# Octonion FFN kernel: another order of the opening steps, and GpSimd's pairing of the last chunks in two steps

## What is computed

```python
W = weights[condition]
y = einsum('bct,bcd->bdt', x, W)
def ternary_dequant(W):
    scale = mean(abs(W))
    return scale * clip(round(W / scale), -1, 1)
def oct_ternary_linear(xp, W):
    M = einsum('jik,jod->koid', S_OCT, ternary_dequant(W))
    return einsum('...id,koid->...ko', xp, M)
h = silu(oct_ternary_linear(y, w_gate)) * oct_ternary_linear(y, w_up)   # 8 x 341.5 -> 2732 wide
out = x + oct_ternary_linear(h, w_down)
```

## Time and profile before

| | before |
|---|---|
| median of 3 runs | 679.83 us (679.83 to 680.08) |
| the profiled execution | 679.09 us |
| its span | 677.3 us |
| TensorE (PE) busy | 643.8 us, 95% of the span |
| VectorE (DVE) | 516.5 us, 76% |
| GpSimd (POOL) | 385.1 us, 57% |
| ScalarE (ACT) | 323.2 us, 48% |
| TensorE's mean granted clock | 0.986 of full |

### The profile page before, as it was taken

One profiled execution on the slowest core, in us unless ns is written; L12 is line 12 of the kernel. 1 busy time (PEld: TensorE's weight loads), 2 busy tenths in 40 slices (PEclk: granted clock), 3 DMA queues, 4 the chain that ended last, 5 costly groups with the idle time before them and its releaser, 6 DMA issues. The chain is left out here.

```text
span 677.3 us, 17118 instructions
## 1 busy us (share of the span) xinstructions
PE 643.8 (95%) x7010; PEld 595.5 (88%) x7010; DVE 516.5 (76%) x873; ACT 323.2 (48%) x542; POOL 385.1 (57%) x453
## 2 busy tenths in 40 slices
PE   3599899999999999999999999999999999999997
PEld 3378699899999999998998999999999999988986
DVE  1899977868776787868877698767878687787785
ACT  4847455345534545254454446254462545434440
POOL 1256685547637576348646476376754486465553
PEclk9799899999999999999999999999999999999997
DMA  9200030140003200041001300031000300021001
GB/s 345 67 2 1 1 116 15 39 155 1 2 2 102 90 2 2 1 137 55 2 2 61 132 1 2 1 126 68 1 2 6 121 1 2 2 72 55 2 1 63
DMA packets 10576, 31.50 MB, mean 47 GB/s; under 512 B 3330, under 2 KB 3330, under 8 KB 10370
## 3 DMA queue, kind: packets, MB, share of 16 engines
q1 hardware_dynamic: 9906, 28.81, 12.3%
q10 hardware_dynamic: 592, 1.61, 0.7%
HBM read 22.02 MB, written 8.39 MB: 45 GB/s over the span
## 5 line engine op out<-in xcount | busy, mean ns | idle before, releaser
L1240 PE MATMUL ps<-y_op,gate_table 128*128 128x256 f16 x1408 | 182.6, 275 | 8.2 <-DVE y_op L979 4.2
L1240 PE MATMUL ps<-y_op,up_table 128*128 128x256 f16 x1408 | 180.3, 273 | 0.2 <-ACT up_table L724 0.2
L1240 PEld LDWEIGHTS ps<-y_op,gate_table 128*128 128x128 f16 x1408 | 138.3, 99 | 27.3 <-issue 4.4
L1240 PEld LDWEIGHTS ps<-y_op,up_table 128*128 128x128 f16 x1408 | 137.9, 98 | 16.8 <-DVE up_table L895 0.7
L617 POOL TENSOR_TENSOR h_pairs<-h_f 128x256 f32<-128x256 f32 (+2 forms) x128 | 118.0, 949 | 60.0 <-ACT h_f L767 57.7
L524 POOL TENSOR_TENSOR o_sb<-o_sb,wd_sb 128x256 f32<-128x256 f32 (+1 forms) x150 | 87.4, 617 | 90.8 <-DVE wd_sb L1108 89.6
L617 POOL TENSOR_TENSOR z_f<-h_pairs 128x512 f32<-128x512 f32 (+1 forms) x80 | 103.7, 1317 | 43.0 <-DVE z_op L995 41.2
L1248 PE MATMUL ps<-third_table,y_op 128*128 128x170 f16 x1408 | 108.2, 237 | 0.6 <-ACT third_table L724 0.6
L1248 PEld LDWEIGHTS ps<-third_table,y_op 128*128 128x128 f16 x1408 | 105.1, 97 | 1.1 <-issue 0.8
L822 ACT ACTIVATE ps<-ps,small 128x512 f32<-128x512 f32 x64 | 42.4, 662 | 111.0 <-DVE ps L1009 85.0
L1401 PE MATMUL ps<-down_u,z_op 128*128 128x256 f16 (+1 forms) x768 | 92.8, 277 | 2.0 <-DVE z_op L995 2.0
(11 more groups left out here) (98 smaller groups left out, 643.2 us busy)
## 6 DMA issues: line engine op xcount, KB each, us to landing
x_in<-in_x_dram SPq DMA_DIRECT2D x8, 1024.0 KB, 5.1
o_sb<-in_x_dram SPq DMA_DIRECT2D x16, 512.0 KB, 3.7
out_dram<-o_sb SPq DMA_DIRECT2D x15, 512.0 KB, 2.7
h_op<-in_L_ffn_w_gate_dram ACTq DMA_DIRECT2D x3, 512.0 KB, 6.8
h_op<-in_L_ffn_w_up_dram SPq DMA_DIRECT2D x3, 512.0 KB, 7.4
z_op<-in_L_ffn_w_down_dram SPq DMA_DIRECT2D x1, 1536.0 KB, 11.4
out_dram<-o_sb SPq DMA_DIRECT2D x2, 256.0 KB, 2.2
cond_bd<-in_L_cond_weights_dram SPq DMA_DIRECT2D x30, 16.0 KB, 3.0
```

The lines of the kernel that those rows point to most:

```text
L1240: mm = pe.matmul(dst, table[m][:, slot, q, :], y_op[:, op, e, :], start=(i == 0 and e == 0), stop=(i == len(terms) - 1 and e == 1))
```

## The change

`pair_up` can do one of its two parts alone; GpSimd's round 4 uses that. It waits for chunks 8 and 9, pairs them, waits for chunks 10 and 11, and pairs those. The other rounds stay as they are. In the opening, ScalarE's sum of up's second window goes to VectorE, where it stands with that of the third window in front of `y_scales`; ScalarE's sum of down's weights goes behind up's table copies; `h_scales(0)` goes behind y's low halves; and TensorE takes gate's total behind the first round of y instead of the second. The counts that the sums wait for change with it.

```diff
@@ -466,13 +466,13 @@
         def z_of(k):
             return (z_dve if k == NR - 1 else z_f)[0:ROWS[k // 2]]
 
-        def pair_up(add, k, pairs):
+        def pair_up(add, k, pairs, parts=(0, 1)):
             w, v = divmod(k, 2)
             n_rows = ROWS[w]
             for r0 in range(2):
                 signs = [KAPPA[2 * a + 1 + 4 * v] * parity(r0) for a in range(2)]
-                a_runs = [(slice(0, 2), signs[0])] if signs[0] == signs[1] else [
-                    (slice(a, a + 1), signs[a]) for a in range(2)]
+                a_runs = [(slice(0, 2), signs[0])] if signs[0] == signs[1] and len(parts) == 2 else [
+                    (slice(a, a + 1), signs[a]) for a in parts]
                 for a, sign in a_runs:
                     c = 4 * w + 2 * a.start
                     n = a.stop - a.start
@@ -671,10 +671,18 @@
 
             def round_of_z(T, k):
                 n = (NR - 1) * T + k
-                pool.wait_ge(h_copied, NC * T + 4 * (k // 2) + 4)
-                if n > 0:
+                if k == NR - 2:
+
+                    pool.wait_ge(h_copied, NC * T + NC - 2)
                     pool.wait_ge(z_ready, n)
-                pair_up(signed_add, k, h_pairs).then_inc(pairs_ready, 1)
+                    pair_up(signed_add, k, h_pairs, (0,))
+                    pool.wait_ge(h_copied, NC * T + NC)
+                    pair_up(signed_add, k, h_pairs, (1,)).then_inc(pairs_ready, 1)
+                else:
+                    pool.wait_ge(h_copied, NC * T + 4 * (k // 2) + 4)
+                    if n > 0:
+                        pool.wait_ge(z_ready, n)
+                    pair_up(signed_add, k, h_pairs).then_inc(pairs_ready, 1)
                 pool.wait_ge(pairs_ready, n + 1)
                 if k > 0:
                     pool.wait_ge(z_lo_ready, NR * T + k)
@@ -857,12 +865,11 @@
                 sum_abs_of(0, w)
             for r in range(4):
                 copy_y(0, r)
-            for w in range(NQ - 1):
-                sum_abs_of(1, w)
+            sum_abs_of(1, 0)
             y_hi(0)
+            copy_slots(1, 0)
             act.wait_ge(down_loaded, 16)
-            sum_abs(2 * NQ - 1, raw_down_at, NQ * raw_n, abs_sum[2])
-            copy_slots(1, 0)
+            sum_abs(NQ + 1, raw_down_at, NQ * raw_n, abs_sum[2])
 
             corr_list = [(w, run) for w in range(NQ) for run in corr_runs]
             per_chunk = -(-len(corr_list) // len(CORR_AFTER))
@@ -1118,17 +1125,18 @@
             scales(0)
             ternary_of(0, 0)
             build_table(0, 0)
+            for w in range(1, NQ):
+                dve.wait_ge(up_loaded[w], 16)
+                dve.tensor_reduce(abs_sum[1][:, w:w + 1], raw[1][w].rearrange("p j o -> p (j o)"), AX.X, ALU.add,
+                                  apply_absolute_value=True).then_inc(abs_summed_dve, 1)
             y_scales(0)
-            dve.wait_ge(up_loaded[NQ - 1], 16)
-            dve.tensor_reduce(abs_sum[1][:, NQ - 1:NQ], raw[1][NQ - 1].rearrange("p j o -> p (j o)"), AX.X, ALU.add,
-                              apply_absolute_value=True).then_inc(abs_summed_dve, 1)
             scales(1)
             scales_of_ffn()
-            h_scales(0)
             y_lo(0, range(2))
             ternary_of(1, 0)
             build_table(1, 0)
             y_lo(0, range(2, NY))
+            h_scales(0)
             ternary_of(0, 1)
             for T in range(NT):
                 for c in range(NC):
@@ -1182,9 +1190,9 @@
         @block.tensor
         def _(pe):
             def sum_abs(m):
-                pe.wait_ge(abs_summed, (NQ, 2 * NQ - 1, 2 * NQ)[m])
                 if m == 1:
-                    pe.wait_ge(abs_summed_dve, 1)
+                    pe.wait_ge(abs_summed_dve, NQ - 1)
+                pe.wait_ge(abs_summed, NQ + m)
                 pe.matmul(totals(m), ones[:], abs_sum[m], start=True, stop=True).then_inc(totals_ready, 1)
 
             def mix(i):
@@ -1467,10 +1475,9 @@
                     down_part(s, down_u_of(2), False, True).then_inc(down_u_done, 1)
 
             pe.wait_ge(ones_set, 4)
-            for r in range(2):
-                y_round(0, r)
+            y_round(0, 0)
             sum_abs(0)
-            for r in range(2, 4):
+            for r in range(1, 4):
                 y_round(0, r)
             row_norms(0)
```

## The result

| | before | changed |
|---|---|---|
| median of 7 runs | 679.83 us (677.97 to 680.16) | 675.79 us (675.54 to 677.02) |
| ratio, 95% interval | | 0.9954 (0.9941 to 0.9967) |
| the profiled execution's span | 677.3 us | 674.7 us |
| TensorE's mean granted clock | 0.986 | 0.987 |

The ratio is 3.1 us of 679.8 (2.2 to 4.0). The two medians lie 4.0 us apart, as single executions scatter by 1 to 2 us; the account goes by the ratio. The forecast was 1.3 us. Its wide range, 674.8 to 680.0, held the time; what the forecast case alone allowed, 677.7 to 679.3, did not.

The account below looks back on a forecast made before the run. TensorE, busy 643.8 of 677.3 us, was taken as the bound, so only its idle or half-clock time counts. Opening -1.5 and end +0.2 gave 679.83 - 1.3 = 678.5 us; range 674.8 to 680.0.

Parts of the forecast that it names:

- the forecast case: Whole kernel: opening gains 1.5 us, end loses 0.2, clock falls as before; 678.5 us, chance 0.52.
- the closed gap: Rival, last tile: GpSimd and VectorE overlap better than by turns, clock stays, 674.8 us; chance 0.18.
- the kept clock: Rival, end: TensorE's last gap stays but the clock doesn't fall, 676.2 us; chance 0.12.
- Steps 1 to 4: Opening: gate's total some 1.8 us earlier, up's sums fit on VectorE, 2.4 us wait gone, low halves 2.0 us earlier.
- Steps 1 and 4: Opening: gate's total behind one round of y, some 1.8 us earlier; `h_scales` (0.83 us) leaves the front of the low halves.
- Step 4: Opening: `h_scales` leaves the front of the low halves, which start at 22.5 instead of 24.65; 2.0 us taken.
- the bounds of none and 0.8: Opening, up's products: depending on the clock's return, 1.1 or 1.9 us of the gain is left; 1.5 taken.
- The sum of down: Opening, ScalarE: placed behind up's table copies, it ends at 31.8, just before the copy of q; hidden, almost nothing to spare.
- In tiles 0 to 6 TensorE waits for nothing there: worth nothing.: Middle tiles: GpSimd's round 4 in two steps brings no gain, as TensorE doesn't wait for it.
- the 5.6 of the sum: Last tile: remaining VectorE and GpSimd adds, taken by turns, need 5.6 us from 652.7; end 0.2 us later.
- something came through: Denies the rival that late sum of down or first tile's waits take the whole gain, 679.8 us; chance 0.12.
- The slower one: Rival, every tile: z's low half of round 3 is delayed past 0.59 us to spare, 682.1 us; chance 0.06.

## Why the prediction was right, and where it was not

The range held, but partly by luck. It reached down to 674.8 for two rivals, the closed gap and the kept clock, and neither happened in the profiled execution. What carried the time below the forecast case was a gain at the tile boundaries that the prediction had put at nothing.

**The opening: right.** Steps 1 to 4 held in place and size: the total at 12.8, the sums hidden (0.39 us before the norms), the first high half as what is late next, 2.0 us between norms and chunk 0 gained (8.03 us before, 6.06 after), for a 2.0 forecast. Steps 1 and 4 were undone one at a time and are worth 1.1 and 0.2 us; what is left of the 2.0, 0.7 us, no run took apart. Step 4 is worth so little because VectorE idles 0.61 us in front of the low halves anyway, and the scales take 0.83. Up's products did run partly at half rate, 0.5 us of loss, between the bounds of none and 0.8. So 2.0 us came through, but 0.5 of them are the earlier norms; without these it would be the forecast's 1.5. The sum of down was hidden with 0.7 us to spare. The first tile handed the gain on; its own stretch of half rate (75 to 78.5 us before) did not come after, and no more than 0.3 us came of that.

**The middle tiles: wrong, and the term that failed.** "In tiles 0 to 6 TensorE waits for nothing there: worth nothing." It waited for VectorE's adds at each boundary; 0.35 us a tile, 2.1 us in six. The row was read the earlier trace rows and set aside, since the view named no engine and the pieces were 0.2 us; but they lay at the start of every tile, and each stood for 0.35. That is more than the 1.8 us between the forecast's 1.3 and the measured 3.1; the clock at the end took part of it back.

**The end: right in kind.** The two engines take turns by whole instructions, the gain on GpSimd is lost on VectorE, and the gap stays. The size was off: z's last products 0.2 us later was the forecast, 0.1 us earlier is what the two pairs of kernels with and without the two steps show. VectorE's four adds took 5.16 us from the start of the first to the end of the last, not the 5.6 of the sum: in turn, an add of VectorE takes 0.55 us, one of pairs 0.59 and one of z 1.13, where the sum had 0.6, 0.7 and 1.25. The low half of round 5, blocked for 2.32 us before, took 1.22, as the sum had it.

**The clock: wrong in both directions.** That the stretch at half rate would be as long as it was failed in the profiled execution: it was 3.4 us longer, and took 1.6 us of the gain. And the rivals' price for a clock that stays, 2.7 us over the kernel before, was the time of TensorE's products; behind them stands GpSimd's part of the output, and the kept clock was worth 1.05 us. Where rows of the chain behind a stall aren't followed to the last store, its price is an upper bound.

**The rivals.** The gap didn't close, the clock didn't stay in the profiled run, something came through. The slower one fell by its own point: z's low half of round 3 was held to 1.51 us (1.22 before), 0.3 us of the 0.59, and no middle tile waits.

**What stays open.** From tile 7's start to z's last products the kernels with the new opening take some 0.3 us longer than those with the old (67.92 and 67.66 us with round 4 undivided). It arises at one instruction, a silu of ScalarE in tile 7, which is 0.27 us later counted from the tile's start, and all that hangs on it follows. Before, and in the changed kernel:

```profile
643.91 0.54 ACT L818 ACTIVATE pu_sb<-ps,small 128x340 f32<-128x340 f32 x1 [0.95 <-DVE ps L1019]
...
639.78 0.54 ACT L826 ACTIVATE pu_sb<-ps,small 128x340 f32<-128x340 f32 x1 [1.23 <-issue]
```

All nine profiles with the new opening, whole or in part, have this idle time of 1.20 to 1.24 us without a releaser, all five with the old one 0.93 to 0.95 us with VectorE as releaser. What ScalarE waits for isn't shown; it is a small cost of the new opening far away from it.

The scatter of single runs, some 1 to 2 us, was seen beside different moments of the clock's return and fall, but no run fixed these moments, so it isn't shown that they cause all of it.

## What to carry to other kernels

A wait of 0.2 us without a named engine is worth a look when it recurs at the same place in each pass of a loop: multiply before dismissing, and compare the period of the loop, which can have lost more than the wait shows (0.35 us here). If two engines work on the last items side by side in SBUF with two inputs each, what one gains by starting earlier can be lost on the other, so count both to the last instruction. Fill a last gap of TensorE with products that need nothing late: in all four kernels here it kept the clock, so that gains from elsewhere weren't taken back there.

## What the runs showed of the hardware

GpSimd's and VectorE's adds with two inputs in SBUF exclude each other and take turns by whole instructions: GpSimd's last two pairs of instructions take 1.40 and 2.49 us with VectorE's adds narrowed to a column, beside the full ones 1.92 and 3.27, and in the changed kernel the ends of the two engines' adds alternate. The Trainium skill states it as an exclusive lock (SBUF — State Buffer, "Who interferes with whom"), and the trace agrees.

Unexpected was the granted clock: in the profiled executions it fell to 1.2 GHz behind last gaps of TensorE of 1.56, 1.94, 1.95 and 2.09 to 2.22 us, and stayed at 2.4 GHz through one of 1.81. Where it fell, it was down for 6.8 or 10.2 us. The Trainium skill's page "TensorE: Matmul & The Clock Gate" (section "Why this matters for your kernels") advises against idle gaps of TensorE and names longer ones than these; here a gap of 1.56 us was enough, and the measurement decides.
